# A vision-transformer block on one core: attention normalised before it is turned back, maxima reduced in pairs, another order of the work, and tokens 2p and 2p+1 on one partition

## The chip, the cores and the metric

The kernel runs on one core of a Trainium2 chip. The time is the device time of one execution in microseconds; three runs of the kernel before gave a median of 1737.85 us (1737.76 to 1738.62). Besides TensorE (PE), VectorE (DVE), ScalarE (ACT) and GpSimd (POOL), the queue of SyncE (SP) issues most transfers.

## What is computed

128 images of 224x224x3 are cut into 14x14 patches, embedded in 192 numbers each, and get one class token: 197 tokens an image, padded to 198 in the kernel. Then one transformer block follows:

```
h = concat(cls, patches(x, with four shifted copies) @ W + b)      # 128 x 197 x 192
n = layernorm(h);  q, k, v = n @ Wq.T, n @ Wk.T, n @ Wv.T          # 6 heads of 32
scores = q.k * HD**-0.5 + lam * (q.anchor)   (the same for every key)
h = h + softmax(scores) @ v @ Wo.T
n = clip(round(layernorm(h) / 0.02)) as int8
h = h + (n @ weight_t) * 0.0002 + bias                             # weight_t is int8
```

## The kernel before, in words

`build_tokens` embeds all images, row of patches by row of patches, and leaves h and its normalised form in HBM scratch. `build_attention` then handles the images one by one in a software pipeline. Every engine has its own `step(i)`, called by `images` for i = -5 to 131, and a step works on several images at once: it turns the normalised tokens of image f = i+5, projects q and k of a pair of images p (three blocks of 128 rows: two in an odd step, one in an even step), scores image a = i+1, does the transposed scores and exponentials of b = i, sums values for c = i-1, output projection and residual for e = i-2, and the quantised FFN for g = i-3 and k = i-4. The order inside a step is written out by hand, the same images in each engine's own order, and semaphores are the only link. Each engine executes in order, so an instruction that waits holds up all behind it.

For one image: `score(n, h)` (L899) makes the scores of head h for 99 x 2 queries in `S_BANK[h % 2]`, only to find the largest per query; `maxima(n, h)` (L1189) reduces them on VectorE, one head at a time, so that one bank is read while the other is filled. The negated maxima are split in a high and a low part (`max_parts`), turned (L1077), copied to SBUF by ScalarE (`max_rows`) and sent by a small transfer into the last rows of `q_st`. `score_t` (L913) then makes the transposed scores with the maximum already subtracted, in the one bank `T_BANK`, and `exps` (L1089) writes their exponentials to `probs`. GpSimd (heads 0 to 3) and VectorE (heads 4 and 5, `add_keys`) add the two halves of the keys; `attend` (L927) multiplies with the values and, with `pick`, sums the exponentials. Its output is transposed, features on partitions. ScalarE copies it to `o_t`, TensorE turns it (`turn_back`, L955), VectorE divides by the sums (L1264, L1269: `inv_sum`, `att`), TensorE turns `att` again, and ScalarE and VectorE split that in `a_mix` and `a_lo` for the output projection (`project_output`, L887). Behind it VectorE adds the residual (`h1`, L1257) and takes statistics; GpSimd adds the bias (`hb`), makes the layernorm factors (`pair_factors`, L151 on) and the scaled `qx`; VectorE quantises (L1244, L1247); TensorE turns, ScalarE copies to `qx_t`, TensorE does the FFN (L1007) and VectorE makes `y` (L1239).

SyncE stacks the high and low parts of q and k into `q_st` and `k_st` (`stack`, L762: nine transfers in an odd step, three in an even one), and loads `xn_in` and `h_in` and stores `out`. Token t lies at partition t mod 99, half t div 99.

## Time and profile before

| what | value |
|---|---|
| median of three runs | 1737.85 us |
| span of the profiled execution | 1736.1 us, 53274 instructions |
| PE busy | 1655.0 us, 95% |
| PEld busy (weight loads) | 1504.7 us, 87% |
| DVE busy | 1471.9 us, 85% |
| POOL busy | 925.9 us, 53% |
| ACT busy | 759.4 us, 44% |
| HBM read and written | 126.54 MB and 58.29 MB |

The times in what follows are of the profiled execution; a start is counted from the start of the span. Instructions of one engine overlap, so their lengths add up to more than the engine's busy time, and the distance from one start to the next is what an instruction costs. The image loop fills the span from some 460 us on; 800 to 1200 us is its steady part.

### The profile page before, as it was taken

The numbers are of one execution on the slowest core, as the hardware profiler recorded it, in microseconds if no ns is written. First come the engines' busy times: TensorE is split into PE (matmuls) and PEld (weight loads), VectorE is DVE, ScalarE is ACT, GpSimd is POOL, SyncE is SP. The second block draws the span as 40 slices with busy tenths as digits, with TensorE's granted clock in tenths as the row PEclk, the third lists the DMA queues.
The fourth block names the chain that finished last, engine by engine and source line by source line (L and its number), as shares of the span: only waits on it lengthen the run. The fifth ranks groups of instructions, "written<-read, shape, count | busy, mean of one in ns | idle before, by whom it ended". The sixth has DMA issues, their size and how long they took to land.

```text
span 1736.1 us, 53274 instructions
## 1 busy us (share of the span) xinstructions
PE 1655.0 (95%) x16368; PEld 1504.7 (87%) x16368; DVE 1471.9 (85%) x3906; ACT 759.4 (44%) x1751; POOL 925.9 (53%) x1911
## 2 busy tenths in 40 slices
PE   4999999996699999999999999999999999999996
PEld 4999999996588888888888888888888888888884
DVE  7888888895388988888888888888888888888885
ACT  2000000001265555556565555655556555555653
POOL 3353544536055655555555565556555555555555
PEclk9999999998699999999999999999999999999998
DMA  9999999973777778787887878877787878878771
GB/s 299 265 306 297 314 290 308 314 257 143 123 140 151 142 146 146 148 147 138 148 149 149 145 139 147 150 146 143 143 147 146 150 138 147 147 150 145 139 119 33
DMA packets 216158, 303.66 MB, mean 175 GB/s; under 512 B 47776, under 2 KB 205011, under 8 KB 205988
## 3 DMA queue, kind: packets, MB, share of 16 engines
q1 hardware_dynamic: 204690, 227.17, 65.4%
q10 hardware_dynamic: 7426, 39.47, 7.8%
q0 software_dynamic: 3984, 36.28, 5.3%
q8 instruction: 32, 0.52, 0.1%
q14 instruction: 26, 0.21, 0.0%
HBM read 126.54 MB, written 58.29 MB: 106 GB/s over the span
## 4 chain that ended last, share of the span: by engine, by line
PE 50%; DVE 8%; POOL 7%; issue 7%; DMA 2%; SPq 1%; ACT 0%; ACTq 0%; POOLq 0%; DVEq 0%
PE bank L874 9%; PE o_bank L932 8%; PE bank L922 6%; PE bank L908 6%; PE bank L895 5%; PE bank L883 5%; PE o_bank L855 3%; PE o_bank L951 2%; PE bank L855 2%; PE o_bank L960 2%; POOL ln L163 2%; DVE neg_max L1193 2%; PE bank L1007 2%; DMA k_st<-qk_lo 2%; POOL qx L1369 2%
## 5 line engine op out<-in xcount | busy, mean ns | idle before, releaser
L1093 ACT ACTIVATE probs<-bank 99x396 f32<-99x396 f32 x768 | 381.8, 497 | 217.7 <-PE bank L922 217.4
L1336 POOL TENSOR_TENSOR key_sum<-probs 99x396 f32<-99x396 f32 x256 | 227.4, 888 | 433.5 <-ACT probs L1093 284.5
L1193 DVE TENSOR_REDUCE neg_max<-bank 99x2 f32<-99x394 f32 x768 | 419.4, 560 | 16.4 <-PE bank L908 12.3
L340 PE MATMUL bank<-e_t,xt 128*128 128x192 f32 x2352 | 389.0, 329 | 25.2 <-DVE xt L448 21.5
L340 PEld LDWEIGHTS bank<-e_t,xt 128*128 128x128 f32 x2352 | 387.5, 192 | 26.4 <-DVE xt L448 26.2
L922 PE MATMUL bank<-q_st,k_st 99*99 99x198 f32 x1536 | 280.6, 264 | 5.7 <-DMA q_st<-max_rows 2.9
L908 PE MATMUL bank<-k_st,q_st 96*99 96x198 f32 x1536 | 275.6, 275 | 10.1 <-DMA k_st<-qk_lo 4.1
L448 DVE STREAM_TRANSPOSE xt<-x_t 128x256 f32<-128x256 f32 x588 | 214.9, 416 | 46.0 <-PE bank L340 44.6
L922 PEld LDWEIGHTS bank<-q_st,k_st 99*99 99x99 f32 x1536 | 208.0, 167 | 50.5 <-issue 42.5
L908 PEld LDWEIGHTS bank<-k_st,q_st 96*99 96x99 f32 x1536 | 193.3, 167 | 26.8 <-issue 12.6
L932 PE MATMUL o_bank<-probs,vals 99*32 99x198 f32 (+1 forms) x3072 | 199.0, 337 | 0.0
L1087 ACT ACTIVATE o_t<-o_bank 128x396 f32<-128x396 f32 x128 | 64.1, 501 | 234.9 <-PE o_bank L951 234.9
L932 PEld LDWEIGHTS o_bank<-probs,vals 99*32 99x32 f32 (+1 forms) x3072 | 113.6, 110 | 47.3 <-ACT probs L1093 0.2
L951 PE MATMUL o_bank<-key_sum,pick 99*32 99x198 f32 x1536 | 151.9, 332 | 0.0
L1369 POOL TENSOR_SCALAR qx<-h,ln 99x192 f32<-99x192 f32 x256 | 126.4, 501 | 40.1 <-POOL ln L163 40.1
L1348 POOL TENSOR_TENSOR hb<-h,ffn_bias 99x384 f32<-99x384 f32 x128 | 129.4, 1011 | 3.7 <-DVE h L1257 3.7
L349 ACT ACTIVATE ffn_w_bf<-ffn_raw 96x384 bf16<-96x384 int8 x1 | 0.5, 522 | 294.8 <-DVE xt L448 294.8
L163 POOL TENSOR_TENSOR ln<-ln,minus_half 99x2 f32<-99x2 f32 x128 | 116.0, 906 | 23.1 <-POOL ln L162 23.1
L1210 DVE TENSOR_TENSOR qk_lo<-bank,qk_hi 128x396 fp32r<-128x396 f32 x192 | 108.3, 564 | 19.4 <-ACT qk_hi L1102 18.4
L895 PE MATMUL bank<-wo_hi,a_mix 128*99 128x192 f32 x512 | 120.3, 253 | 0.0
L895 PE MATMUL bank<-wo_lo,a_mix 128*99 128x192 f32 x512 | 120.2, 253 | 0.0
L1102 ACT ACTIVATE qk_hi<-bank 128x396 fp32r<-128x396 f32 x192 | 96.1, 501 | 49.9 <-PE bank L874 43.2
(134 smaller groups left out, 3593.0 us busy)
## 6 DMA issues: line engine op xcount, KB each, us to landing
x_t<-in_x_dram SPq DMA_DIRECT2D x26, 1344.0 KB, 21.9
x_t<-in_x_dram ACTq DMA_DIRECT2D x26, 1344.0 KB, 23.1
q_st<-qk_hi SPq DMA_DIRECT2D x126, 198.0 KB, 4.4
k_st<-qk_hi SPq DMA_DIRECT2D x126, 198.0 KB, 4.4
xn_in<-xn_scratch SPq DMA_DIRECT2D x128, 148.5 KB
h_in<-h_scratch SPq DMA_DIRECT2D x128, 148.5 KB
h_scratch<-h_t POOLq DMA_DIRECT2D x13, 1344.0 KB, 17.2
xn_scratch<-xn_t POOLq DMA_DIRECT2D x13, 1344.0 KB, 8.0
```

What stands on the lines that cost most here:

```text
L340: last = pe.matmul(token_bank(p)[:, 0:D], xt[:, p, c // 3, c % 3, :], e_t[:, row_kind(t), col, c // 3, c % 3, :], start=c == 0, stop=c == 5)
L448: last = nc.vector.transpose(xt[:, p, :, c, :].rearrange("p m (g b) -> p g m b", b=32), pix[:, c])
L874: last = pe.matmul(wide(bank, BLOCK), weights[:, Q:K + 1, :].rearrange("p w n -> p (w n)")[:, cols], inputs, start=i == 0, stop=i == len(p ...
L895: last = pe.matmul(bank[0:TC, c * D:(c + 1) * D], inputs, weights, start=i == 0, stop=i == len(pairs) - 1)
L908: last = pe.matmul(S_BANK[h % 2][0:TC, c * TP:(c + 1) * TP], q_st[0:ST, n.pair, h, n.two, c * TC:(c + 1) * TC], k_st[0:ST, n.pair, h, n.tw ...
L922: last = pe.matmul(T_BANK[0:TC, c * TP:(c + 1) * TP], k_st[:, n.pair, h, n.two, c * TC:(c + 1) * TC], q_st[:, n.pair, h, n.two, :], start= ...
L932: pe.matmul(o_bank[at % 4 * HD:(at % 4 + 1) * HD, 0, col:col + TP], vals[0:kk, n.two, kc, h, :], probs[0:kk, n.two, h, kc, :], start=kc == ...
L951: last = pe.matmul(o_bank[to:to + HD, 0, TP:2 * TP], pick[:, j, :], key_sum[:, n.two, HEAD_AT[side * HG + j], :], start=j == 0, stop=j == ...
L1093: nc.scalar.activation(probs[:, n.two, h, :, :], wide(T_BANK, TC), ACT.Exp).then_inc(exp_done, 1)
L1193: nc.vector.tensor_reduce(out=neg_max[:, n.two, :, h], in_=wide(S_BANK[h % 2], TC)[:, :, 0:NTOK], axis=AX_X, op=ALU.max, negate=True).then ...
L1336: nc.gpsimd.tensor_tensor(key_sum[:, b.two, heads, :], probs[:, b.two, heads, 0, :], probs[:, b.two, heads, 1, :], ALU.add).then_inc(pool_ ...
L1369: nc.gpsimd.tensor_scalar(qx[:, e.two, cc, :], h1[:, e.two, cc, :], v[7][:, cc:cc + 1], v[6][:, cc:cc + 1], ALU.add, ALU.mult).then_inc(ln ...
```

## The change

- Attention is normalised while it is still transposed. The sums of the exponentials are made by TensorE with `ones`, spread over the 32 rows of each head: for heads 0 to 3 from GpSimd's key sums into a second bank, for heads 4 and 5 straight from `probs`. ScalarE takes Ln of them and Exp of the negative (`near`, nearly the reciprocal), and VectorE does one Newton step: `unity` = sum x near, `rough` = values x near, `att_t` = (unity - 2) x rough. This has the opposite sign, which `h1` takes back by subtracting. `o_t`, `turn_back`, the reciprocal, `att` and its turn are gone, and so is VectorE's `add_keys`; `a_lo` is made by GpSimd.
- The scores of two heads stand in a tile of two banks (`s_pair`), and one reduction reads both.
- Every engine has a new order within a step. `score_t` 4 and 5 belong to the step after; `project_values` is for image b, one step later than before; quantising and GpSimd's factors are for q = i-3; turning `qx` and the FFN are for g = i-4; the store of y is for k = i-5, and there is one more drain step. GpSimd no longer waits for the maxima ahead of its second key sum. In an odd step SyncE issues the stackings of block 0, the loads and the store of y ahead of the others.
- Token 2p+c lies at partition p, half c. `xn_in`, `h_in` and `out` follow this.

The core of the diff:

```diff
+        s_pair = ctx.enter_context(nc.psum_tensor("s_pair", [128, 2, 512], F32))
-                by_chunk = xn_dram[n.n].rearrange("(c p) d -> p c d", p=TC)
+                by_chunk = xn_dram[n.n].rearrange("(p c) d -> p c d", c=2)
# score(n, h): waits for max_done once per pair of heads
+                if h % 2 == 0 and (n.reuses(1) or h >= 2):
+                    pe.wait_ge(max_done, n.count(HG, h // 2))
# maxima(n, j): one for two heads
+                dve.wait_ge(scored, n.count(H, 2 * j + 2))
+                both = s_pair[0:TC, :, 0:2 * TP].rearrange("p h (c n) -> p h c n", c=2)[:, :, :, 0:NTOK]
+                nc.vector.tensor_reduce(out=neg_max[:, n.two, :, 2 * j:2 * j + 2].rearrange("p c h -> p h c"), in_=both,
                                         axis=AX_X, op=ALU.max, negate=True).then_inc(max_done, 1)
# attend_first(n): waits for exps 0 to 3, then heads 0 to 3, both halves; attend_rest(n):
+                for kc in range(2):
+                    for h in range(SIDE, H):
+                        add_values(n, h, kc)
+                    for h in range(SIDE, H):
+                        to = (h - SIDE + 2) * HD
+                        last = pe.matmul(O_ROWS[to:to + HD, REST], ones[0:kk, :], probs[0:kk, n.two, h, kc, :],
+                                         start=kc == 0, stop=kc == 1)
+                last.then_inc(av_done, 1)
+                pe.wait_ge(pool_sums, n.count(2, 2))
+                for h in range(SIDE):
+                    last = pe.matmul(SUM_ROWS[h * HD:(h + 1) * HD, FIRST], ones[:], key_sum[:, n.two, h, :],
+                                     start=True, stop=True)
+                last.then_inc(sums_done, 1)
# ScalarE
+            nc.scalar.preload_act_table_set("natural_log_exp_and_others")
+                    nc.scalar.activation(log_sum[0:DB, 1, :], O_ROWS[DB:DA, REST], ACT.Ln).then_inc(log_done, 1)
+                    act.wait_ge(sums_done, c.count(1, 1))
+                    nc.scalar.activation(log_sum[:, 0, :], SUM_ROWS[:, FIRST], ACT.Ln).then_inc(log_done, 1)
+                    nc.scalar.activation(near[:], log_sum[:], ACT.Exp, scale=-1.0).then_inc(near_done, 1)
# VectorE
+                    nc.vector.tensor_tensor(unity[:, 0, :], SUM_ROWS[:, FIRST], near[:, 0, :],
+                                            ALU.mult).then_inc(unity_done, 1)
+                    nc.vector.tensor_tensor(unity[0:DB, 1, :], O_ROWS[DB:DA, REST], near[0:DB, 1, :], ALU.mult)
+                    nc.vector.tensor_tensor(rough[:], wide(O_ROWS, DA), near[:], ALU.mult).then_inc(rough_done, 1)
+                    nc.vector.scalar_tensor_tensor(out=att_t[:], in0=unity[:], scalar=2.0, in1=rough[:],
+                                                   op0=ALU.subtract, op1=ALU.mult).then_inc(att_done, 1)
# GpSimd
+                    nc.gpsimd.tensor_tensor(a_lo[:, e.two, :], att_t[:, 0, :], a_mix[:, e.two, 0, :].bitcast(F32),
+                                            ALU.subtract).then_inc(pool_lo, 1)
```

The orders within a step, before and after (numbers are heads; blocks are those of q and k; "odd" and "even" are the step's):

```
PE before:   score a0 a1 | odd: block 0, score_t c5, block 1 / even: block 2, score_t c5 | score a2 | FFN k | attend c |
             score_t b0 | score a3 | output e | score_t b1 | turn_back c | turn xn f | score a4 | score_t b2 | turn qx g |
             turn att c | score a5 | score_t b3 | values a | score_t b4 | turn maxima a
PE after:    odd: block 0 / even: block 2 | score a0 a1 | score_t c4 | turn qx g | values b | score_t c5 | score a2 a3 |
             odd: block 1 | attend_first c | score_t b0 | FFN g | score a4 a5 | turn xn f | score_t b1 | attend_rest c |
             score_t b2 | output e | score_t b3 | turn maxima a
DVE after:   maxima a01 | low | unity e (0-3) | maxima a23 | att_t e | odd: low 1 | y g | maxima a45 | a_mix e | copy
             max_parts a | x_lo f | quantise q (1) | max_parts a | quantise q (2) | h1 e | unity c (4, 5) | bn e | rough c
ACT after:   high | exp c4 | qx_t g | exp c5 | vals b | odd: high 1 | exp b0 | a_mix e | x_hi f | exp b1 | Ln c | Ln c |
             exp b2 | near c | max_rows a | exp b3
POOL after:  factors q | key sum c (2, 3) | qx q (2 halves) | a_lo e | key sum b (0, 1) | hb e
SP after:    odd: block 0 high x2 | xn | h_in e | y k | block 1 high x4 | low x3 | maxima a
             even: xn | block 2 x3 | h_in e | y k | maxima a
```

## Rows read from the trace of the kernel before

**Rows 1.** Busy us of each engine in a stretch (x instructions), TensorE's granted clock, transfers.

```profile
core 0: us, PE busy (x) PEld busy (x) DVE busy (x) ACT busy (x) POOL busy (x), PEclk, DMA share, GB/s
800.00:1200.00 400.00, 396.38 (x4471) 351.89 (x4470) 355.41 (x920) 235.57 (x552) 234.78 (x492) 1.00 0.79 145
```

**Rows 2.** Line 1244 in 800 to 1200 us: duration ns min/median/max, first and last start.

```profile
L1244 DVE TENSOR_SCALAR qx<-qx x41: 346/360/361, 807.7 to 1199.5; 99x384 f32<-99x384 f32 x41
```

**Rows 3.** Timeline of TensorE: start us, us, line, op, out<-in, merged neighbours.

```profile
1000.00 0.36 PE L874 MATMUL bank<-x_hi,wa_hi 128*128 128x396 f32 x1
...
1000.94 0.34 PE L908 MATMUL bank<-k_st,q_st 96*99 96x198 f32 x2
...
1001.54 1.04 PE L932 MATMUL o_bank<-probs,vals 99*32 99x198 f32 x18
1002.25 0.34 PE L951 MATMUL o_bank<-key_sum,pick 99*32 99x198 f32 x2
...
1003.36 0.43 PE L922 MATMUL bank<-q_st,k_st 99*99 99x198 f32 x2
...
1003.81 0.26 PE L895 MATMUL bank<-wo_hi,a_mix 128*99 128x192 f32 x1
...
1004.72 0.34 PE L922 MATMUL bank<-q_st,k_st 99*99 99x198 f32 x2
1004.90 0.60 PE L960 MATMUL o_bank<-ident,o_t 128*99 128x128 f32 x4
1005.34 0.51 PE L855 MATMUL bank<-ident,xn_in 99*128 99x99 f32 x4
1005.63 0.41 PE L908 MATMUL bank<-k_st,q_st 96*99 96x198 f32 x2
...
1006.42 0.56 PE L855 MATMUL o_bank<-ident,att 99*128 99x99 f32 x4
1006.76 0.41 PE L908 MATMUL bank<-k_st,q_st 96*99 96x198 f32 x2
...
1007.19 0.26 PE L883 MATMUL bank<-wa_hi,x_hi 128*99 128x192 f32 x1
...
1008.12 0.34 PE L922 MATMUL bank<-q_st,k_st 99*99 99x198 f32 x2
```

**Rows 4.** Timeline of VectorE in the same step.

```profile
1001.98 0.56 DVE L1193 TENSOR_REDUCE neg_max<-bank 99x2 f32<-99x394 f32 x1
1002.46 0.56 DVE L1210 TENSOR_TENSOR qk_lo<-bank,qk_hi 128x396 fp32r<-128x396 f32 x1
...
1003.48 0.36 DVE L1244 TENSOR_SCALAR qx<-qx 99x384 f32<-99x384 f32 x1
...
1005.54 0.23 DVE L1264 RECIPROCAL inv_sum<-o_bank 99x12 f32<-99x12 f32 x1
...
1006.76 0.62 DVE L1279 TENSOR_TENSOR x_lo<-bank,x_hi 128x198 fp32r<-128x198 f32 x2
...
1008.18 0.61 DVE L1297 BATCH_NORM_STATS2 st<-h 99x6 f32<-99x192 f32 x2
1008.71 0.35 DVE L1304 TENSOR_TENSOR a_lo<-o_bank,a_mix 128x198 fp32r<-128x198 f32 x1
```

**Rows 5.** Waits of VectorE in 800 to 1200 us: total us, times, longest.

```profile
DVE qx L1244 <- POOL qx L1369: 12.4, 13, 1.0
```

**Rows 6.** Groups by line of ScalarE over the whole span: busy us, mean ns, idle before.

```profile
L349 ACT ACT_TABLE_LOAD x1 | 1.3, 1283 | 2.1 <-issue 2.1
```

**Rows 7.** Timeline of SyncE's queue in a step with two blocks.

```profile
1001.11 1.24 SPq L762 DMA_DIRECT2D q_st<-qk_hi  x2
...
1009.23 0.67 SPq L752 DMA_DIRECT2D q_st<-max_rows  x1
```

**Rows 8.** Line 163 over the whole span: duration ns min/median/max, first and last start.

```profile
L163 POOL TENSOR_TENSOR ln<-ln,minus_half x128: 703/976/1132, 491.4 to 1727.7; 99x2 f32<-99x2 f32 x128
```

**Rows 9.** Timelines of VectorE and GpSimd at 1011 us.

```profile
1011.03 0.56 DVE L1200 TENSOR_TENSOR key_sum<-probs 99x396 f32<-99x396 f32 x1
...
1011.03 1.12 POOL L163 TENSOR_TENSOR ln<-ln,minus_half 99x2 f32<-99x2 f32 x1 [0.18 <-POOL ln L162]
```

More of the change, by code:

```diff
@@ L665, in build_attention @@
     key_rows = tile("key_rows", [ST + 3, TP])
[L666 to L669 removed]
+    key_sum = tile("key_sum", [TC, NS, SIDE, TP])
+    log_sum = tile("log_sum", [DA, 2, TP])
+    near = tile("near", [DA, 2, TP])
+    unity = tile("unity", [DA, 2, TP])
+    rough = tile("rough", [DA, 2, TP])
+    att_t = tile("att_t", [DA, 2, TP])
     a_mix = tile("a_mix", [DA, NS, 2, TP], F32R)
@@ L730, in images @@
                 step(At(k, r, MOD))
-        for i in range(last, B + 4):
+        for i in range(last, B + 5):
             step(At(0, i, MOD))
```

530 lines of the change are left out of this document (239 added, 291 removed).

## Prediction

> **What bounds the kernel now.** I read the busy time by stretch first, then the period of the image loop, then the order of work on TensorE and on VectorE in two neighbouring steps, and last the waits. In the steady stretch TensorE is busy 396 of 400 us, VectorE 355, ScalarE 236 and GpSimd 235 [rows 1]. Matmuls overlap, so that 396 does not say that TensorE never waits; the start times must be read. One step of the loop handles one image: forty-one quantisations lie between 807.7 and 1199.5 us, so a step takes 391.8 / 40 = 9.80 us [rows 2]. With 128 steps the loop is 1254 of the 1736.1 us, and the token stage ahead of it is touched only in which bank it names. Everything is therefore decided by the step: 0.01 us of it is 1.28 us of the total.
>
> TensorE, from start to start [rows 3]: a projection block takes 0.94 us (1000.00 to 1000.94) and comes three times in two steps, 1.41 a step; a pair of score matmuls 0.18 (1004.72 to 1004.90), twelve pairs, 2.16; one such pair and the FFN take 0.60 (1000.94 to 1001.54), so the FFN 0.42; attend 1.82 (1001.54 to 1003.36); the output projection 0.91; turning o_t back 0.44; turning xn 0.29, and qx, of as many turns, about the same; turning att 0.34; the values 0.93; turning the maxima, two turns, about 0.15. The sum is 9.16, of 9.80. TensorE waits some 0.6 us a step.
>
> VectorE, start to start [rows 4]: a reduction of 394 columns is 0.56 us long and the next instruction starts 0.48 after it; a 396-wide two-input operation is as long. So an instruction costs its length less an overlap of 0.08: the two 198-wide x_lo, 0.62 together, 0.54; the two bn_stats, 0.61, 0.53; one quantising step is 0.36 long and the second waits for it, 0.68 for both; a_lo is 0.35 long and also has a wait ahead, 0.36; the reciprocal, 0.23 long with a dependent multiplication behind it, about 0.27. A step has six maxima (2.88, and 0.1 for a dependent wait), 1.5 lows (0.72), key_sum, y, h1 and att (1.92), the reciprocal 0.27, x_lo 0.54, quantising 0.68, the two small max_parts about 0.30, bn 0.53, a_lo and the low part of a_mix 0.72: 8.66. So VectorE too is idle for only 1.1 us, of which 12.4 us in 41 steps, 0.3 a step, is for the quantiser that GpSimd feeds [rows 5]. Two engines of 9.2 and 8.7 us of work, each waiting for the other in a hand-written order, make 9.8.
>
> **The change, part by part.** *TensorE.* Normalising before the turn drops turn_back (0.44) and the turn of att (0.34): -0.78. Attend had 18 real matmuls, 36 records, in 1.82; the first 18 records took 0.71, 0.039 each, since four column tiles run side by side [rows 3]. After it there are 8 matmuls in attend_first and 12 in attend_rest, 40 records, all in groups of four tiles: 40 x 0.04 = 1.6, a gain of about 0.2. (The old third group used two tiles of four.) TensorE comes to 9.16 - 0.78 - 0.2 = 8.2. If nothing fills the four tiles, 40 records at the old mean of 0.05 are 2.0 and the sum is 8.6.
>
> *VectorE.* A 198-wide operation is 0.35 long and a 396-wide one 0.56, so 198 columns cost 0.21 us, and a reduction of 788 columns is 0.56 + 0.42 = 0.98 long, the next start 0.90 after it [rows 4]. Three are 2.70 against 2.98: -0.28. Were a pair to cost as much as two, the sum would be 0.2 higher. Removed: key_sum 0.48, reciprocal 0.27, att 0.48, a_lo 0.36 (to GpSimd): -1.59. Added: unity in two parts of 198 columns 0.27 each, rough 0.48, att_t 0.48: +1.50. The result is 8.66 - 0.37 = 8.3. The sign turned in h1 is free. So VectorE gains little, and becomes the busiest engine.
>
> *ScalarE.* It drops o_t (0.50) and gains two Ln of 198 columns and one Exp of 396, some 0.3 + 0.3 + 0.5: 5.8 busy becomes 6.4 of some 9. This is covered, except by order: exps(b,2) stands behind both Ln, which wait for the last sum matmul, and score_t(b,3) waits for exps(b,2). TensorE meanwhile has score_t 2 and the output projection, 0.18 + 0.91, against Ln and Exp of about 0.3 + 0.4 + 0.1 after the sums. No stall there, without much over. The trace has one table load of 1.28 us, at the start [rows 6]; the change's preload puts in one more, about 1.3 us once.
>
> *GpSimd.* a_lo moves here. The nearest row is a key sum, 0.89 us for twice the input columns, so about 0.5; ends 0.35 (VectorE's price) and 0.89. GpSimd goes from 5.7 to 6.2 us a step. Its chain now runs from h1 through hb (1.0), the factors (2.9), one key sum (0.9), qx (1.0) to the quantiser of the next step, about 6.1 us, and the quantiser, h1 included, adds some 1.4: a loop of 7.5, below 8.3. The 0.3 us a step that VectorE now waits for GpSimd [rows 5] should go; late next is pool_lo, on which the output projection waits.
>
> *Order.* The maxima share one pair of banks, so score(a,2) cannot start before the first pair is reduced, where before the next head had its own bank. I laid the new orders side by side, with zero where the first pair of scores is issued. VectorE: first maxima 0.3 to 1.2, low to 1.7, unity to 1.95. TensorE: score_t 4, qx, values and score_t 5 take 0.18 + 0.29 + 0.93 + 0.18, then scores 2 and 3 end at about 2.0, readable at 2.3. So VectorE waits 0.35 for the second maxima. Then maxima to 3.2, att_t 3.7, y 4.2, last maxima 5.1 (scores 4 and 5 were issued at 3.3 to 3.7), a_mix 5.5, copy 5.7, x_lo 6.2, quantising with the small max_parts 7.0, h1 7.5, unity 7.75, bn 8.3, rough 8.8, and the next maxima start then: 8.5 us for a step with one block, 9.0 with two (low for block 1 is 0.48 more), 8.75 in the mean. TensorE's own chain needs 0.6 less in a one-block step and about as much in the other. Waits between engines that this walk does not see were 9.80 - 8.66 - 0.86 = 0.3 in the old loop, if the listed waits of VectorE (35 us in 41 steps, 12.4 of them in [rows 5]) are 0.86. Taking nearly that again gives 8.75 + 0.25 = 9.0 us a step.
>
> *Transfers.* SyncE issues as many DMAs as before; a pair of stacking DMAs holds its queue for 1.24 us, and in a two-block step it starts at 1001.11 and reaches the row of maxima at 1009.23 [rows 7]. Nine stackings of 0.62 and six others of about 0.4 are 8.0 us: it fits into 9, with less to spare than in 9.8. The new token order joins the two pieces of h_in and of out into one of twice the length, the rest keeps its pieces. I count that at nothing, since the transfers do not show up as releasers on the steady stretch; if the queues did get late, the start of a step would wait for its stacked operands. The extra drain step stores the last image and does no new work: nothing to 1 us.
>
> **A rule weighed.** The power operation on GpSimd takes 0.70 us at least and 1.13 at most, and it took 1.12 at 1011.03, where VectorE started a key_sum with both inputs in SBUF [rows 8, 9]. Somebody's read held it back by 0.4 us. The Trainium skill, SBUF — State Buffer, Practical consequences, says that a VectorE instruction with two SBUF inputs contends with a GpSimd instruction that reads SBUF, and that whichever was issued second is blocked fully. The row agrees for one direction; no row here shows VectorE held by GpSimd. That direction is rival 2.
>
> **Forecast** (0.52): 9.0 us a step. 128 x 0.80 = 102 us off the profiled 1736.1, 1634; the median of the runs lies 1.75 above the span, so 1636. Own range 8.7 to 9.3: 1597 to 1674.
>
> **Rival 1, the waits vanish** (0.13): both engines are at their sums and the step is 8.3 to 8.6. For it: the new order spreads the producers away from their consumers. Against it: the pair of banks. 8.45 gives 1736.1 - 173 + 1.75 = 1565.
>
> **Rival 2, GpSimd holds VectorE** (0.20). By the walk att_t, both inputs in SBUF, starts at 3.2, where GpSimd is at its key sum (3.1 to 4.0), and the low part of a_mix at 5.5, where it is at the other (5.3 to 6.2). If each waits it out, 0.6 + 0.3 or so is added: 9.0 + 0.6 (some of it in place of other waits) = 9.6, and 1736.1 - 26 + 1.75 = 1712. Speaking against it: if VectorE is first, GpSimd waits 0.4, which its loop can bear. The same price would come from the shared banks, were the 0.35 to become 0.9.
>
> **Rival 3, slower** (0.10): the two functions do not stay in one table. Each step would then load twice, at 1.28 [rows 6], between the sums and exps(b,2), where the walk leaves TensorE no slack: 9.0 + 2.6 = 11.6 us, 1968. It decides from the first load inside the loop; a single load a step (10.3) would already lose. A milder form is an order in which ScalarE's Ln wait holds up exps, from 0.8 us a step on. For it: ScalarE waits in order, and the two Ln are the first instructions there that wait for the end of attend with an exp behind them. Against it: the table that is preloaded is named for both functions. The Trainium skill, ScalarE: Activation LUTs, Table sets, lists one set with both; no row of before shows it.
>
> The rest (0.05) is a step within 0.02 us of the old one or just around it. The change doing what it says is not in doubt for the removed turns; for the paired maxima its failure is priced above. A measurement can tell about 0.2% here, 3.5 us. Faster by more 0.87, within 0.03, slower 0.10. The range reaches from 8.58 us a step, inside rival 1, to 9.65 at the far end of rival 2: 1582 to 1719; outside are most of rival 1, and rival 3.
>
> **What would show it.** TensorE's records of turn_back and att gone, attend in 1.6 to 2.0; a paired reduction of 0.98 (right if 0.95 to 1.0, wrong if over 1.05); VectorE busier than now, above 90%, its longest wait the second maxima on TensorE; no table load in the loop; a_lo on GpSimd about 0.5, and not the last releaser of the output projection. Wrong is the forecast if VectorE is idle over 1 us a step, if att_t starts when a GpSimd key sum ends, or if the score matmuls wait for stacked operands.

## The result and the profile after

The changed kernel takes 1814.0 us (median of 4 runs, 1810.0 to 1815.7) against 1737.8: a ratio of 1.044, 95% interval 1.0425 to 1.0455. The forecast was 1636. It is slower, and by a mechanism that is none of the rivals. A few executions (one each of e14 and e16 below, one of the kernel before) ran slower at a lower granted clock, and the ratios leave them out.

The page of the kernel after, its head, the chain that ended last, and three groups of part 5 (busy us and mean ns | idle before and its releaser):

```profile
span 1813.1 us, 52082 instructions
PE 1634.8 (90%) x15856; PEld 1408.1 (78%) x15856; DVE 1524.3 (84%) x3521; ACT 874.4 (48%) x2008; POOL 1064.2 (59%) x2039
...
DMA 17%; SPq 17%; PE 14%; DVE 13%; issue 11%; POOL 2%; ACT 1%; DVEq 1%; ACTq 0%; POOLq 0%
...
L1185 DVE TENSOR_REDUCE neg_max<-s_pair 99x4 f32<-99x788 f32 x384 | 374.1, 974 | 20.4 <-PE s_pair L912 20.3
L1309 POOL TENSOR_TENSOR key_sum<-probs 99x396 f32<-99x396 f32 x256 | 308.5, 1205 | 102.3 <-ACT probs L1079 73.9
...
L1272 DVE TENSOR_TENSOR h<-h_in,bank 99x384 f32<-99x384 f32 x128 | 70.5, 551 | 115.8 <-DMA h_in<-h_scratch 109.8
```

The chain has 17% of the span in DMA landings, nearly all of it (16%) the landing of `h_in`, and 17% in SyncE's queue. The last row names VectorE's longest wait, 109.8 us over the span, in front of `h`, which before waited for no transfer. Busy time in the steady stretch (the columns are those of [rows 1]), and the waits there that concern TensorE and VectorE:

```profile
800.00:1200.00 400.00, 368.33 (x4082) 302.03 (x4074) 349.64 (x752) 257.26 (x600) 262.79 (x500) 1.00 0.74 138
```

```profile
DVE h L1272 <- DMA h_in<-h_scratch: 34.4, 19, 2.0
...
PE s_pair L912 <- DVE neg_max L1185: 13.6, 19, 0.7
...
DVE y L1230 <- PE bank L1025: 7.5, 19, 0.4
...
PE s_pair L912 <- DMA k_st<-qk_lo: 4.8, 17, 0.5
```

In the list of waits each line gives the engine and what it made, what it waited for, and the total, the times and the longest in us. Against [rows 1] TensorE has lost 28 us of busy time in 400 and VectorE 6, and the transfers' share fell from 0.79 to 0.74. ScalarE and GpSimd are busier (257 and 263 us against 236 and 235), at 66% or less: no engine is full, and the two that set the pace before wait. The length of a step is read here from the 128 rows of maxima that ScalarE copies, first and last start of them:

```profile
L1073 ACT ACTIVATE max_rows<-bank x128: 324/325/329, 459.9 to 1774.8; 12x198 fp32r<-12x198 f32 x128
```

(1774.8 - 459.9) / 127 = 10.35 us a step; before it was 9.82 by the same rows (456.4 to 1703.4), 9.80 by [rows 2]. The step of one block shows where it goes, in SyncE's queue and at VectorE:

```profile
1003.93 0.72 SPq L756 DMA_DIRECT2D q_st<-max_rows  x1
1004.95 0.93 SPq L773 DMA_DIRECT2D xn_in<-xn_scratch  x1
1006.08 0.88 SPq L774 DMA_DIRECT2D xn_in<-xn_scratch  x1
1007.06 1.28 SPq L766 DMA_DIRECT2D k_st<-qk_hi  x2
1008.39 0.61 SPq L766 DMA_DIRECT2D k_st<-qk_lo  x1
1009.19 0.39 SPq L818 DMA_DIRECT2D h_in<-h_scratch  x1
```

```profile
1014.14 0.55 DVE L1272 TENSOR_TENSOR h<-h_in,bank 99x384 f32<-99x384 f32 x1 [1.77 <-DMA h_in<-h_scratch]
```

(SPq is SyncE's queue; its second number is how long the issue of the transfer holds the queue, "x2" two of them.) Two things are new. `h_in` is issued at 1009.19 for the `h` of the very same step; by the chain it lands 4.87 us later, and VectorE sits idle for 1.77. And the two loads of `xn_in`, which before took 0.34 and 0.30 us of SyncE's time, take 0.93 and 0.88, with the stacking of k and `h_in` queued behind them.

### The profile page after: what moved, and what is told of

The parts are those of the page before. It is cut to its first block, busy times and chain, and to the rows that moved or that the text cites. A ratio compares the mean times of both kernels' runs of the same rounds, so it can differ in the third digit from the quotient of the medians.

```text
span 1813.1 us, 52082 instructions
## 1 busy us (share of the span) xinstructions
PE 1634.8 (90%) x15856; PEld 1408.1 (78%) x15856; DVE 1524.3 (84%) x3521; ACT 874.4 (48%) x2008; POOL 1064.2 (59%) x2039
## 4 chain that ended last, share of the span: by engine, by line
DMA 17%; SPq 17%; PE 14%; DVE 13%; issue 11%; POOL 2%; ACT 1%; DVEq 1%; ACTq 0%; POOLq 0%
DMA h_in<-h_scratch 16%; SPq L766 7%; PE bank L878 4%; DVE neg_max L1185 4%; SPq L773 3%; SPq L774 3%; PE o_bank L934 3%; PE s_pair L912 2%; SPq L756 2%; DVE h L1272 2%; DVE rough L1284 2%; DVE x_lo L1249 2%; PE bank L926 2%; DVE st L1281 1%; PE bank L1025 1%
## 5 line engine op out<-in xcount | busy, mean ns | idle before, releaser
L1185 DVE TENSOR_REDUCE neg_max<-s_pair 99x4 f32<-99x788 f32 x384 | 374.1, 974 | 20.4 <-PE s_pair L912 20.3
L1309 POOL TENSOR_TENSOR key_sum<-probs 99x396 f32<-99x396 f32 x256 | 308.5, 1205 | 102.3 <-ACT probs L1079 73.9
L926 PE MATMUL bank<-q_st,k_st 99*99 99x198 f32 x1536 | 298.1, 275 | 4.9 <-ACT probs L1079 4.6
L912 PE MATMUL s_pair<-k_st,q_st 96*99 96x198 f32 x1536 | 228.6, 271 | 62.2 <-DVE neg_max L1185 45.4
L926 PEld LDWEIGHTS bank<-q_st,k_st 99*99 99x99 f32 x1536 | 196.5, 166 | 87.8 <-ACT probs L1079 44.3
L912 PEld LDWEIGHTS s_pair<-k_st,q_st 96*99 96x99 f32 x1536 | 176.3, 168 | 95.4 <-DVE neg_max L1185 57.0
L934 PE MATMUL o_bank<-probs,vals 99*32 99x198 f32 (+1 forms) x3072 | 226.1, 340 | 0.0
L1272 DVE TENSOR_TENSOR h<-h_in,bank 99x384 f32<-99x384 f32 x128 | 70.5, 551 | 115.8 <-DMA h_in<-h_scratch 109.8
L956 PE MATMUL o_bank<-probs,ones 99*32 99x198 f32 (+1 forms) x1024 | 112.2, 340 | 0.0
L899 PEld LDWEIGHTS bank<-wo_hi,a_mix 128*99 128x99 f32 x512 | 85.3, 167 | 32.5 <-issue 32.5
## 6 DMA issues: line engine op xcount, KB each, us to landing
xn_in<-xn_scratch SPq DMA_DIRECT2D x128, 148.5 KB
h_in<-h_scratch SPq DMA_DIRECT2D x128, 148.5 KB
h_scratch<-h_t POOLq DMA_DIRECT2D x13, 1344.0 KB, 18.3
```

What stands on the lines that cost most here:

```text
L899: last = pe.matmul(bank[0:TC, c * D:(c + 1) * D], inputs, weights, start=i == 0, stop=i == len(pairs) - 1)
L912: last = pe.matmul(s_pair[0:TC, h % 2, c * TP:(c + 1) * TP], q_st[0:ST, n.pair, h, n.two, c * TC:(c + 1) * TC], k_st[0:ST, n.pair, h, n.tw ...
L926: last = pe.matmul(T_BANK[0:TC, c * TP:(c + 1) * TP], k_st[:, n.pair, h, n.two, c * TC:(c + 1) * TC], q_st[:, n.pair, h, n.two, :], start= ...
L934: pe.matmul(O_ROWS[at * HD:(at + 1) * HD, cols], vals[0:kk, n.two, kc, h, :], probs[0:kk, n.two, h, kc, :], start=kc == 0, stop=kc == 1)
L1185: nc.vector.tensor_reduce(out=neg_max[:, n.two, :, 2 * j:2 * j + 2].rearrange("p c h -> p h c"), in_=both, axis=AX_X, op=ALU.max, negate=T ...
L1309: nc.gpsimd.tensor_tensor(key_sum[:, n.two, heads, :], probs[:, n.two, heads, 0, :], probs[:, n.two, heads, 1, :], ALU.add).then_inc(pool_ ...
```

## The experiments

Times are medians of four to ten executions. Each ratio, with its 95% interval in parentheses, is to the kernel before, measured beside it. Differences in us are between medians; where kernels were not measured side by side the ratios are the safer guide, and the text says where that matters. "Step" is worked out as above, and "the stretch" is 800 to 1200 us.

**The two suspects, singly and together.** The edit of e1: `h_in` is loaded one step earlier again.

```diff
-                f, p, a, e, k, ahead = i.plus(5), pair_of(i), i.plus(1), i.plus(-2), i.plus(-5), i.plus(7)
+                f, p, a, c, k, ahead = i.plus(5), pair_of(i), i.plus(1), i.plus(-1), i.plus(-5), i.plus(7)
...
-                if e.within(B):
+                if c.within(B):
```

> The changed kernel with one edit: SyncE loads h_in for image c = i-1 in each step, one step ahead of its use, as the kernel before did, and no longer for e = i-2 in the step that uses it. Theory L (late load): VectorE's wait for h_in, 34.4 us in 39 steps of 800 to 1200 us, 0.88 a step, goes, and most of it is gained, 0.6 to 0.88 us a step of 10.37, so 1814 becomes 1700 to 1737. Rival Q (the queue of SyncE is the bound, its issues of xn_in having grown from 0.34 and 0.30 to 0.93 and 0.89 us): the wait only moves to the stacked operands and the step stays above 10.1, so 1780 or more.

Measured: 1766.2 us, 1.018 (1.016 to 1.0201), step 9.97: between the two theories, and each is right in part. VectorE's wait for `h_in` is gone; the wait of TensorE for the stacked k grew from 4.8 to 18.3 us in the stretch:

```profile
PE s_pair L912 <- DMA k_st<-qk_lo: 18.3, 20, 1.1
```

The edit of e2: tokens laid out as before, `(c p)` in place of `(p c)`, in the loads of `xn_in` (shown) and `h_in` and the store of `out` (not shown); nothing else.

```diff
-                by_chunk = xn_dram[n.n].rearrange("(p c) d -> p c d", c=2)
+                by_chunk = xn_dram[n.n].rearrange("(c p) d -> p c d", p=TC)
```

> The changed kernel with the old token layout in the loads of xn_in and h_in and the store of out (token t at partition t mod 99), everything else as changed. Theory T (the layout makes the xn_in issues long): they return to 0.34 and 0.30 us, h_in is issued 1.2 us earlier in the step, and its wait of 1.8 us in every second step falls to 0.6 or less: 0.6 us a step, 1735 to 1750. Rival M (the layout's merged pieces help the transfers, and long issues cost nothing): 1814 or more, since h_in and out return to pieces of half the length.

Measured: 1741.7, 1.0039 (1.0025 to 1.0053), step 9.79. e3 has both edits.

> The changed kernel with both edits: h_in loaded one step ahead, and the old layout. If the late h_in is the whole of what SyncE does to this kernel, this is as fast as the earlier load alone (within 10 us), about 1700. If the long issues of xn_in also delay the stacked operands or the row of maxima, it is faster than the earlier load alone by 0.1 to 0.4 us a step, 13 to 50 us.

Measured: 1715.2, 0.9884 (0.9866 to 0.9902), step 9.57. So the late `h_in` costs 48 us beside the new layout (1814 to 1766) and 27 beside the old one (1741.7 to 1715.2); the layout costs 72 and 51. (The kernel after was not measured beside e1 and e2; by the ratios the 48 and 72 are 45 and 70.) With both undone the rest of the change is faster than before by 20 us. e4 is the reverse: the kernel before with the new layout alone.

> The kernel before with nothing but the new layout (token 2p+c at partition p, half c, in the loads of xn_in and h_in and the store of out). Theory T: its xn_in issues grow to about 0.9 us each, SyncE has 1.2 us more in a step; in a two-block step its queue was busy for all but some 0.7 us up to the row of maxima, so that row goes out some 0.5 us late in every second step: 1738 becomes 1750 to 1780. Theory M: fewer packets, 1738 or less.

Measured: 1799.4, 1.0366 (1.0346 to 1.0385), step 10.30. The layout alone makes the old kernel 64 us slower, more than the 12 to 42 expected. The issues are the same and so is the wait, for the stacked k and not for the row of maxima as the expectation had it:

```profile
1005.02 0.94 SPq L769 DMA_DIRECT2D xn_in<-xn_scratch  x1
1006.16 0.86 SPq L770 DMA_DIRECT2D xn_in<-xn_scratch  x1
```

```profile
PE bank L909 <- DMA k_st<-qk_lo: 16.4, 19, 1.4
```

e5 keeps the new layout (on e1) but loads each half `c` with transfers of its own, four in place of two.

```diff
-                sp.dma_start(xn_in[:, n.slot % NX, :, 0:D], by_chunk).then_inc(xn_landed[n.slot], 16)
-                sp.dma_start(xn_in[:, n.slot % NX, :, D:DA + 2 * DB], by_chunk[:, :, DA:D]).then_inc(xn_landed[n.slot], 16)
+                for half in range(2):
+                    sp.dma_start(xn_in[:, n.slot % NX, half, 0:D], by_chunk[:, half, :]).then_inc(xn_landed[n.slot], 16)
+                    sp.dma_start(xn_in[:, n.slot % NX, half, D:DA + 2 * DB], by_chunk[:, half, DA:D])\
+                        .then_inc(xn_landed[n.slot], 16)
```

> The new token layout and h_in one step ahead (1766 us so far), with the two transfers into xn_in cut into four, one for each half c, so that neither side of a transfer interleaves the halves. If the long issue of xn_in (0.94 and 0.86 us) comes from the two halves of neighbouring tokens in one transfer, each of the four takes 0.30 to 0.35 us, 1.3 us together and some 0.2 us between them: about what the two took, and the time stays within 10 us of 1766. If the layout's long issue comes from the alternating rows in HBM themselves, each of the four is 0.5 or more, SyncE gets later still, and the time is above 1780.

Measured: 1743.4, 1.0041 (1.0027 to 1.0055), 23 us less than e1, where about none were expected. Each of the four is short (two are shown, the others take 0.30):

```profile
1003.73 0.33 SPq L774 DMA_DIRECT2D xn_in<-xn_scratch  x1
1004.25 0.31 SPq L775 DMA_DIRECT2D xn_in<-xn_scratch  x1
```

The same bytes from the same alternating rows of HBM are issued in four times 0.3 us. The long issues are those in which one transfer takes both halves of a token pair, adjacent rows of HBM, to places that lie apart in SBUF; `h_in`, contiguous on both sides, stayed at 0.3 to 0.4. Why the issue takes longer the runs don't show. The gain fits the queue: from the first issue of `xn_in` to the next transfer SyncE needs 2.20 us in e1 (1010.15 to 1012.35), 1.99 in e5 (1003.73 to 1005.72) and 1.07 in e3 (1008.84 to 1009.91). The 0.2 us between e1 and e5 are 0.16 us a step (9.97 against 9.81), with the bytes the same; the rest of the layout's price, 28 us between e5 and e3, has 0.9 us of queue time beside it.

**GpSimd and VectorE.** In the kernel after, the copy of 12 columns into `max_parts` and the two-input `att_t` stand against GpSimd's key sums, which take 0.89 alone:

```profile
1001.34 0.90 POOL L1309 TENSOR_TENSOR key_sum<-probs 99x396 f32<-99x396 f32 x1 [0.37 <-ACT probs L1079]
1007.75 1.50 POOL L1309 TENSOR_TENSOR key_sum<-probs 99x396 f32<-99x396 f32 x1 [0.24 <-POOL ln L163]
```

```profile
1001.52 0.75 DVE L1243 CAST max_parts<-neg_max 99x12 fp32r<-99x12 f32 x1
1007.94 0.56 DVE L1220 SCALAR_TENSOR_TENSOR att_t<-unity,rough 128x396 f32<-128x396 f32 x1
```

The first ends with the key sum, 1002.27 against 1002.24, though alone it takes 0.17; the second is not lengthened, and the key sum that runs beside it is, to 1.50. e6 (on e3) lets GpSimd's `add_keys(b, 0)` wait for the second quantising step, so that it does not run under the small copies.

```diff
+                    if q.within(B):
+                        pool.wait_ge(quant_done, q.count(2, 2))
                     add_keys(b, 0)
```

> The old layout and h_in one step ahead (1715 us), and GpSimd starts its second key sum (heads 0 and 1 of b) only when VectorE has quantised. Theory G (GpSimd's key sum holds VectorE's copy into max_parts, 0.63 us against 0.17 before, and the quantiser, 0.44 against 0.36): both return to 0.17 and 0.36, VectorE has 0.5 us a step less, and 1715 becomes 1650 to 1670. Rival: another engine takes over at once, above 1695; or the later key sum makes hb and the factors late and brings a wait for qx, 1715 or more.

Measured: 1706.6, 0.9823 (0.9802 to 0.9844), step 9.51: 9 us, not 50. The copy is short again (median 0.18 over the span, in e3 0.75), so the mechanism was there; the time did not follow, and the rival "another engine takes over at once" holds:

```profile
1000.37 0.17 DVE L1242 CAST max_parts<-neg_max 99x12 fp32r<-99x12 f32 x1
```

**What sets the remaining 9.5.** Three edits of e6: e7 leaves out the second quantising step on VectorE (0.34 us a step); e11 leaves out the two products with `wo_lo` on TensorE (0.36 a step); e12 both. The edits of e7 and e11:

```diff
-                if has_q:
-                    dve.wait_ge(quant_done, q.count(2, 1))
-                    nc.vector.tensor_scalar(qx[:, q.two, :, :], qx[:, q.two, :, :], MAGIC + 127.0, MAGIC - 128.0,
-                                            ALU.min, ALU.max).then_inc(quant_done, 1)
```

```diff
-                    pairs = ((wo_hi[:, 0, :], hi), (wo_lo[:, 0, :], hi), (wo_hi[:, 0, :], lo), (wo_hi[:, 1, :], mix),
-                             (wo_lo[:, 1, :], mix))
+                    pairs = ((wo_hi[:, 0, :], hi), (wo_hi[:, 0, :], lo), (wo_hi[:, 1, :], mix))
```

> As the gated kernel, and the second quantising step on VectorE (the limits -128 and 127) is left out, so one instruction of 0.36 us, 0.28 from start to start, is missing from each step. If VectorE's own work sets the step, it is 0.2 to 0.3 us a step faster than the gated kernel, 25 to 38 us. If TensorE or the orders do, less than 10 us.

> As the gated kernel, with the two products of wo_lo left out of the output projection, 4 matmuls of ten a step, 0.36 us on TensorE; VectorE's work is unchanged. If TensorE sets the step, 0.25 to 0.36 us a step, 32 to 46 us faster than the gated kernel. If the coupling of the orders or VectorE does, less than 15 us.

> e6_key_sum_gated with less work on both engines at once: VectorE's second quantising step (0.34 us a step, the limits of -128 to 127) is left out, and so are the two products with wo_lo of the output projection (4 of 10 matmuls, 0.36 to 0.4 us a step), so the output is not the reference's. Each alone was worth 2 and 6 us of 1706.6. If TensorE and VectorE hold each other (each waits for the other where its own work was cut), both cuts together give 0.25 to 0.35 us a step, 30 to 45 us: about 1665 to 1675. If what is left is the chain of SyncE's order and the landing of the stacked k, the two cuts give no more than their sum, 8 us or less: 1698 or above.

Measured: 1704.3 (0.9809; 0.978 to 0.9839), 1700.5 (0.9803; 0.9787 to 0.9819) and 1696.6 (0.9759; 0.9739 to 0.9779). The cuts give 2, 6 and 10 us by the medians; the intervals of the first two overlap with that of e6, so only the third is clear of noise. Either engine, or both, may do a third of a microsecond less a step (some 45 us in all) and almost nothing follows. Their own work does not set the step of e6. The chain of e11 leads, in this step, through SyncE's queue (start us, us, what):

```profile
1012.39 0.67 SPq L756
...
1013.35 0.33 SPq L773
1013.88 0.33 SPq L774
...
1014.97 0.59 SPq L766
1015.61 6.30 DMA k_st<-qk_lo
```

The row of maxima, then `xn_in`, then the stacking of k, then its landing for 6.30 us. It is not so in every step: TensorE waits for k in 8 of some 42 steps of the stretch in e11, and DMA landings and SyncE's queue together are 26% of the chain in e6 and 19% in e11. Three edits of the orders followed: e8 (on e6) puts the FFN ahead of `attend_first`, e10 (on e6) issues `xn_in` behind the stacking of k in the steps with one block, e9 (on e6) takes one reduction per head in place of the pair. TensorE's order in e8, SyncE's in e10, and VectorE's reductions in e9:

```diff
-                if has_c:
-                    attend_first(c)
-                if has_b:
-                    score_t(b, 0)
                 if has_g:
...
+                if has_c:
+                    attend_first(c)
+                if has_b:
+                    score_t(b, 0)
```

```diff
-                if ahead.within(B):
+                if ahead.within(B) and not (usual and not odd):
                     load_xn(ahead)
...
                     stack(p, k_st, 1, k_last, qk_lo[:, 2, :])
+                    if ahead.within(B):
+                        load_xn(ahead)
```

```diff
-                nc.vector.tensor_reduce(out=neg_max[:, n.two, :, 2 * j:2 * j + 2].rearrange("p c h -> p h c"), in_=both,
-                                        axis=AX_X, op=ALU.max, negate=True).then_inc(max_done, 1)
+                for side in range(2):
+                    dve.wait_ge(scored, n.count(H, 2 * j + 1 + side))
...
+                    nc.vector.tensor_reduce(out=neg_max[:, n.two, :, 2 * j + side],
+                                            in_=wide(s_pair[:, side, :], TC)[:, :, 0:NTOK],
+                                            axis=AX_X, op=ALU.max, negate=True).then_inc(max_done, 1)
```

> As the gated kernel, with the FFN on TensorE ahead of attend_first instead of behind score_t(b,0), so that it is done some 1 us earlier in a step. VectorE's wait for it ahead of y, 9.3 us in 42 steps, 0.22 a step, should go: 15 to 28 us faster than the gated kernel if VectorE sets the step. Rival: score_t(b,0) and the exponentials behind it come later and cost as much, within 8 us.

> As the gated kernel, with SyncE loading xn_in behind the three stackings of block 2 in an even step, not ahead of them, so that these go out 1.0 us earlier. TensorE's wait for the stacked k, 4.5 us in 42 steps, should go: 0.1 us a step, 8 to 14 us faster, if TensorE sets the step. Rival: the wait hid another one (the row of maxima, 4.7 us in 42 steps), within 5 us.

> As the gated kernel (1707 us), with the maxima of each head reduced by an instruction of its own again, in the same place of VectorE's order, and each half of s_pair freed by itself. If TensorE's own work now sets the step (8.98 us by its start times in the gated kernel, of 9.51), the 0.2 to 0.3 us that this adds to VectorE cost nothing or up to 15 us, and the finer hand-over may win some of it back. If VectorE sets the step, 25 to 40 us slower.

Measured: e8 1728.4 (0.9958; 0.9946 to 0.9971), 22 us slower, as TensorE then waits for `vals` (13.6 us in the stretch). e10 1717.2 (0.9889; 0.9868 to 0.991), 11 slower: the wait for k is gone, and TensorE waits for the row of maxima instead, 19.3 us in the stretch where e6 had 4.7. Both are slower than their forecasts and their rivals allowed. e9 1701.0 (0.9803; 0.9787 to 0.982), the lowest median of a complete kernel here, though its interval overlaps with e6's: the paired maxima bring nothing that can be measured. In e10 the row, 9.3 KB, is issued at 1002.43 and TensorE gets it at 1007.02:

```profile
1007.02 0.43 PE L927 MATMUL bank<-q_st,k_st 99*99 99x198 f32 x2 [1.08 <-DMA q_st<-max_rows]
```

**Order of issues or the DMA engines?** e13 (on e6) lets ScalarE issue `xn_in`, e17 (on e9) lets ScalarE issue the row of maxima; both relieve SyncE's queue and move the same bytes. (The first fence is e13's edit, the second e17's.)

```diff
                 has_p = p.within(B)
+                if i.plus(7).within(B) and not (i.fixed and i.n < 0):
+                    load_xn(act, i.plus(7))
                 if has_p and odd:
```

```diff
                 if has_b:
                     exps(b, 3)
+                if has_a and not leads(a):
+                    store_max_rows(act, a)
```

> e6_key_sum_gated with one edit: the two transfers of xn_in are issued by ScalarE, at the start of its step, in place of SyncE between the first stackings and the later ones; bytes and packets stay as they are. SyncE's queue gets 0.64 us a step shorter and the stacking of k no longer stands behind them; ScalarE is 48% busy. If the order of issues on SyncE's queue sets the step, the wait for k_st goes and the step falls by 0.2 to 0.5 us: 1645 to 1680. If the DMA engines themselves set it (they are busy 0.86 of the time), the same bytes land as late as before: 1700 to 1710. If ScalarE's own order suffers from the two issues (exps behind them), it is slower than 1710.

> e9_single_maxima, complete, with one edit: the row of maxima is sent by ScalarE, behind exps(b, 3), and not by SyncE at the end of its step. It is issued about 0.5 us later than SyncE does when SyncE is free, but stands in no queue behind the nine stackings, xn_in, h_in and out. If the row is late because of what stands ahead of it in SyncE's queue, its landing falls from 4 to 6 us to 2 to 3 and the step by 0.1 to 0.4 us: 1650 to 1688. If all queues share the DMA engines alike, it lands as late and, issued 0.5 later, costs up to 60 us: 1700 to 1760.

Measured: 1898.0 (1.094; 1.092 to 1.096) and 1815.7 (1.0456; 1.0391 to 1.0521), the slow branches of both expectations, e17 beyond its 1760. It is not ScalarE's order, as e13's expectation had it for that branch: ScalarE waits for TensorE there (82.7 us for scores in the stretch). The stackings were issued sooner (in a two-block step the last is issued 6.9 us after the first, 7.8 in e6), and the small row behind them landed later. From the chain and the timelines of ScalarE's queue and TensorE in e13:

```profile
1010.03 6.28 DMA q_st<-max_rows
```

```profile
1009.94 0.30 ACTq L763 DMA_DIRECT2D xn_in<-xn_scratch  x1
1010.40 0.31 ACTq L764 DMA_DIRECT2D xn_in<-xn_scratch  x1
```

```profile
1016.43 0.43 PE L925 MATMUL bank<-q_st,k_st 99*99 99x198 f32 x2 [2.73 <-DMA q_st<-max_rows]
```

What the 2.73 us of idling brought with it, in the stretches before and behind it (columns of [rows 1]; the clock is the number before the transfers' share):

```profile
1009.00:1013.70 4.70, 4.70 (x54) 4.10 (x52) 4.55 (x10) 3.13 (x8) 3.60 (x9) 1.00 0.95 140
1016.43:1023.70 7.27, 7.27 (x55) 5.94 (x56) 3.26 (x9) 3.41 (x8) 1.50 (x2) 0.53 0.49 82
```

The granted clock is 1.00, TensorE then stands still, and for the next 7.3 us it is 0.53 in the mean, most of it the lower level of 1.2 GHz: the output projection takes 1.66 us there and 0.91 in the step before. By these rows an estimate: the stall costs itself and about half of 7.3 us again, some 6 in all. In e17 the row had the queue to itself and still took (chain of e17)

```profile
1167.40 4.95 DMA q_st<-max_rows
1189.77 6.42 DMA q_st<-max_rows
```

The chains show what the row's landing goes with: how close to it the first transfer of `xn_in` (148.5 KB) is issued. In e3, on one queue, `xn_in` follows 0.87 to 0.88 us behind the row, and the three rows on the chain land after 3.8 to 3.9 us. In e17 it follows after 0.45 to 0.50 in three steps (the row lands after 4.9 to 5.0) and between 0.15 before and 0.20 behind the row in five (5.9 to 6.4). In e13 ScalarE issues it within 0.3 us of every such row, on either side (5.2 to 6.5). So both edits did more than change queues: they brought a large load up to the small transfer that TensorE needs first. No run moves the queue and keeps that distance, so neither question at the head of this part is answered by e13 or e17.

e14, e13 with the maxima of e9, was no different from e13:

> e13_xn_on_scalar_queue with the maxima of e9_single_maxima (one reduction for each head, halves of s_pair freed singly). e9 was 6 us faster than e6. If the two gains are independent it is e13 less 6 us. If with a free queue TensorE's score matmuls wait for the pair of banks more than before, the single maxima bring more, 10 to 25 us; if VectorE is by then the bound (six instructions of 0.48 to 0.5 in place of three of 0.9, 0.2 to 0.3 us a step more), they cost 5 to 20 us.

Measured: 1900.4 (1.0928; 1.0888 to 1.0967). e15 and e16 leave every issue and wait of e6 in its place and take bytes away; all but 3 of 99 partitions of `h_in`, in e16 also of `xn_in`, keep old data. The edit of e15:

```diff
-                    sp.dma_start(h_in[:, c.two, :, :], h_dram[c.n].rearrange("(c p) d -> p c d", p=TC))\
+                    rows = TC if c.fixed and c.n < NS else FEW
+                    sp.dma_start(h_in[0:rows, c.two, :, :], h_dram[c.n].rearrange("(c p) d -> p c d", p=TC)[0:rows])\
```

> e6_key_sum_gated, but from the third image on h_in is loaded for 3 of its 99 partitions only (the rest keeps what the first two images left, so the output is not the reference's). Issues, waits and their order on SyncE's queue stay; a step moves 144 KB of about 1440 and 192 of about 1546 packets less. In e13 a free queue did not help, and the row of maxima, 9.3 KB, took 6.28 us to land. If the DMA engines' backlog (share 0.86) sets the step, it falls by 0.3 to 0.6 us: 1630 to 1668, with a DMA share of 0.80 or less. If the order on TensorE and VectorE sets it, 1698 or above.

> e15_h_in_few_rows with the same done to both transfers of xn_in (3 partitions from the fourth image on), so that a step moves 336 KB and 576 packets less than e6; the issues on SyncE's queue get shorter if their price goes with what they carry. If the DMA engines' backlog sets the step, TensorE's own sum is next: 9.0 us and a little, 1640 to 1655, below e15. If not, 1698 or above, as e15.

Measured: 1691.1 (0.9734; 0.9718 to 0.975) and 1679.9 (0.9667; 0.9648 to 0.9686), steps of 9.39 and 9.31. Both fell between their two branches: the transfers do hold the step, by 0.20 us of its 9.51, not by the 0.5 that would reach TensorE's own sum (9.0, below). It may not be their bytes alone: the three issues got shorter too, in a two-block step 0.31, 0.28 and 0.25 us against 0.38, 0.33 and 0.30 in e6, and the two were not held apart. In e16 no wait for a transfer is left on TensorE, and it is busy 393 of 400:

```profile
800.00:1200.00 400.00, 393.26 (x4532) 336.71 (x4527) 374.63 (x840) 284.06 (x667) 282.67 (x561) 1.00 0.69 116
```

e18 takes the `wo_lo` products out of e16, to see whether TensorE's own work is the rest.

> e16_xn_h_few_rows and, beside it, the two products with wo_lo of the output projection left out (4 of 10 matmuls, 0.36 us a step on TensorE). On e6, with full transfers, this cut gave 6 us. In e16 no wait for a transfer is left on TensorE, and it is busy 393 of 400 us. If TensorE's own work sets what is left, the cut gives 0.25 to 0.36 us a step, 30 to 46 us: 1634 to 1650. If VectorE (375 of 400 busy) or the order of the two sets it, it gives under 12: 1668 or above.

Measured: 1683.4 (0.9699; 0.968 to 0.9717), no gain. Most of the freed time came back as a wait in front of the output projection (first e16, then e18):

```profile
PE bank L901 <- POOL a_lo L1341: 5.9, 22, 0.3
```

```profile
PE bank L900 <- POOL a_lo L1340: 17.3, 33, 1.0
```

So with slim transfers TensorE waits for GpSimd's `a_lo`, whose order is hb, factors, qx, `a_lo`, behind a key sum that since e6 waits for VectorE. Whether that gate (the wait for the quantiser that e6 added) or GpSimd's work itself closes this loop was not separated: e16 without the gate was not run. What sets the last 0.3 us, 9.31 against 9.0, stays open.

## Why the prediction was wrong

**Where it failed: transfers counted at nothing.** The prediction added up SyncE's step with "six others of about 0.4" and found that it "fits into 9". It did not price one transfer under its new access pattern, and no row of before could: the two loads of `xn_in` take 1.81 us together and not 0.64. It allowed that late queues would show as score matmuls waiting for stacked operands, and gave that no chance. The layout is worth 51 to 72 us (e2, e3) and, alone on the old kernel, 64 (e4); e5 shows with the same bytes that the time of issue is part of it. The prediction's argument, that transfers are no releasers in the steady stretch before, tells that they had been in time, not by how much.

**A move that was overlooked.** The load of `h_in` changes from image i-1 to i-2, which is the image whose `h` is made in the same step. The diff shows it, the prediction does not mention it: 27 to 48 us (e1, e3). In the step shown landing takes 4.87 us, half a step.

Together the two are 10.35 against 9.57 us a step, 99 us of the 178 between forecast and result. The forecast's 9.0 stays 0.57 away. It was VectorE's walk and some waits; the runs show that TensorE's own work alone takes 9.0 (below), that transfers hold 0.2 of the rest (e16) and collisions of GpSimd with VectorE at most 0.06 (e3, e6), and leave 0.3 open.

**TensorE's sum, 9.16 before and 8.2 after.** The removed turns are gone as said, but both sums were too low, because the pairs of score matmuls were all priced by the cheapest row, 0.18. Before, from FFN to FFN:

```profile
1001.12 0.49 PE L1007 MATMUL bank<-ffn_w_bf,qx_t 96*99 96x192 bf16 x4
...
1010.35 0.49 PE L1007 MATMUL bank<-ffn_w_bf,qx_t 96*99 96x192 bf16 x4
```

That is 9.23 us for a step with one block; the one ahead of it, with two, begins with an FFN at 991.12 and takes 10.00. No wait of TensorE is listed in either, so its own work was 9.6 of 9.80, and it waited 0.2 us a step, not 0.6. In the step of two blocks the twelve pairs take 2.5 us, not 2.16. In e6's step of two blocks, which begins at 1003.74, three pairs take (a line of q_st,k_st, to the start of the next line)

```profile
1005.63 0.35 PE L925 MATMUL bank<-q_st,k_st 99*99 99x198 f32 x2
1005.82 0.54 PE L911 MATMUL s_pair<-k_st,q_st 96*99 96x198 f32 x4
...
1008.02 0.43 PE L925 MATMUL bank<-q_st,k_st 99*99 99x198 f32 x2
1008.29 0.49 PE L1024 MATMUL bank<-ffn_w_bf,qx_t 96*99 96x192 bf16 x4
...
1009.29 0.40 PE L925 MATMUL bank<-q_st,k_st 99*99 99x198 f32 x2
1009.62 0.36 PE L933 MATMUL o_bank<-probs,vals 99*32 99x198 f32 x2
```

0.19, 0.27 and 0.33: a pair behind attend or behind transposes costs half as much again or more. The trace of before has it too (the pair at 1003.36 in [rows 3] starts 0.27 ahead of the next matmul), and it was not used. Attend is 0.81 + 1.15 = 1.96, at the far end of the 1.6 to 2.0. The step of two blocks is 9.49 us long, with no wait on TensorE listed inside it, and a block takes 1.0, so the mean step is 9.49 - 0.5 = 9.0: the forecast of 9.0 left TensorE no wait at all. The gain on this engine is about 0.6 (9.6 to 9.0), not 0.96. e18 shows that this sum alone is not the last bound.

**VectorE's sum, 8.3.** The paired reduction is 0.974 (0.98 forecast, right). The rest was some 0.4 low: VectorE is busy 8.7 us a step in e6 (366.0 of 400 us, step 9.51), just as before (355.4, step 9.80), so the change took no work off it. Part of this: where a wait for a semaphore stands ahead of an instruction, the overlap of 0.08 that the sum takes off each length is lost (in e18's VectorE, the last maxima start at 1017.83 and `a_mix` at 1018.83, 1.00 apart and not 0.90). e7, where 0.34 us less work on VectorE gave nothing clear of noise, shows that it cost little.

**The paired maxima** were to bring 0.28 us a step on VectorE. e9 without them is no slower (6 us faster by the medians, within the intervals). The walk's doubt that `score(a, 2)` waits for the pair of banks holds in the kernel after, 13.6 us in the stretch; in e6 that wait is not listed.

**GpSimd's `a_lo`** takes 0.66 in the mean, inside 0.35 to 0.89 and above the 0.5 taken.

**The rivals.** Rival 1 (8.3 to 8.6): not reached even with the transfers cut (9.31). Rival 2 put its price on `att_t` and `a_mix`; `att_t` is not held (0.56) and `a_mix` hardly (median 0.36, 0.42 at most in the stretch). The small copy and the first quantising step are (medians in the stretch 0.57 for the latter, 0.36 before), and e6 prices it at 9 us. Rival 3 fell: one table load more, at 1283 ns, and none in the loop; Ln takes 0.33 to 0.34 us, `near` 0.53. The Trainium skill, ScalarE: Activation LUTs, Table sets, lists one set with both exp and ln; the trace agrees. Two of the signs named at the end as speaking against the forecast came: VectorE idle over 1 us a step (50 us in 39 steps) and score matmuls waiting for stacked operands. `a_lo` is a last releaser of the output projection, 5.1 us in the stretch after and 17.3 in e18.

## What to carry to other kernels

Treat every transfer whose access pattern or place in its queue changes as a new instruction with an unknown price, and follow each moved load to its consumer: issue, landing, use, all in one step's timeline. Hardly any wait listed on a transfer does not tell how much time is to spare: here, at a DMA share of 0.79, some 1.1 us more of issue time a step cost 64 us (e4). Ask of each landing what it stands behind, and what is issued beside it. When two edits give nothing on two engines that are over 90% busy, take away bytes before taking away more work.

## What the runs showed of the hardware

- Issue time depends on the shape: 0.93 and 0.88 us for a load that fills two halves of an SBUF row, which lie apart, from adjacent HBM rows, and 0.3 for each half alone (e5), though the packets of a step went down with the layout, from some 1540 (e3) to 1320 (e1).
- A small transfer on a queue of its own was not early. The Trainium skill, DMA: Bandwidth & Descriptors, Queues, rings and completion order, says that a DMA engine takes turns between its queues packet by packet. By that alone the row of 9.3 KB on ScalarE's queue would pass SyncE's backlog; where the chain of e17 runs through it (8 steps in and at the edge of the stretch), it took 4.88 to 6.42 us, against 3.8 to 3.9 on SyncE's queue in e3 and 4.4 to 4.7 in e10. Its landing went with the distance to the load of 148.5 KB issued nearest: 3.8 to 3.9 us at 0.87, 4.9 to 5.0 at 0.45 to 0.50, 5.9 to 6.4 at 0.2 or less. (In the step of e10 shown, the load comes 3.3 us later, but two stackings of k, 198 KB each, begin 0.90 behind the row.) Whether the distance is the cause was not tested.
- VectorE against GpSimd, both ways. The Trainium skill, SBUF — State Buffer, Practical consequences, says that VectorE's copies and casts in its 2-port mode, and its instructions with two SBUF inputs beside a GpSimd instruction that reads SBUF, contend with GpSimd, and that the one issued first decides: the other is blocked fully. The copy of 12 columns agrees (0.17 alone, 0.75 under a key sum begun before it). `att_t`, with both inputs in SBUF and begun 0.19 us after the key sum, does not: it keeps its 0.56, and the key sum that was first is lengthened from 0.89 to 1.50. The measurement decides: a two-input operation of VectorE was not held here, and GpSimd paid. GpSimd's power operation, 0.98 in the median in [rows 8], takes 0.70 in the kernel after, where VectorE's key sum is gone.
- A stall of 2.7 us on TensorE was followed by 7.3 us at a granted clock of 0.53, which by the estimate above made a wait of 2.7 us a loss of some 6. Over the stretch the granted clock is 0.88 in e13 and 1.00 in e6, and TensorE's waits for the row are 39.0 us against 4.7; e13 is 9% slower than before by both together.
